# First mixture of experts: three pieces of side work take other places among the expert products

## The reference, cut to what matters

```python
def _L0_ffn_ref(x, gate_w, gate_b, w1, b1, w2, b2, gamma, beta):
    B, S, H, F, E, K = (8, 1024, 64, 128, 16, 2)
    gate_logits = x @ gate_w + gate_b
    topk_vals, topk_idx = jax.lax.top_k(gate_logits, K)
    topk_w = jax.nn.softmax(topk_vals, axis=-1)
    h = jax.nn.relu(jnp.einsum('bsh,ehf->bsef', x, w1) + b1)
    expert_out = jnp.einsum('bsef,efh->bseh', h, w2) + b2
    sel = jnp.take_along_axis(expert_out, topk_idx[:, :, :, None], axis=2)
    moe = jnp.sum(topk_w[..., None] * sel, axis=2)
    y = x + moe
    mu = jnp.mean(y, axis=-1, keepdims=True)
    var = jnp.var(y, axis=-1, keepdims=True)
    return (y - mu) / jnp.sqrt(var + EPS) * gamma + beta
...
    h = h + _L0_ffn_ref(_layernorm(h, axis=-1), ...)
    h = h + _L1_attn_ref(_layernorm(h, axis=-1), ...)
```

```python
    pos_score = (rel @ Wpos.T + bpos).transpose(2, 0, 1)
    pos_score = jax.nn.softmax(pos_score, axis=-1)
```

## Time and profile before

| | us |
|---|---|
| median of 3 runs | 759.2 (756.96 to 759.57) |
| profiled execution | 761.38 |
| its span, first to last instruction | 759.6 |
| from the first `sum_turn` (chunk 1) to the last of the eight chunks' (chunk 7) | 315.84 to 447.49 |

### The profile page before, as it was taken

One profiled execution on the slowest core, in us unless ns is written; L12 is line 12 of the kernel. 1 busy time (PEld: TensorE's weight loads), 2 busy tenths in 40 slices (PEclk: granted clock), 3 DMA queues, 4 the chain that ended last, 5 costly groups with the idle time before them and its releaser, 6 DMA issues.

```text
span 759.6 us, 16399 instructions
## 1 busy us (share of the span) xinstructions
PE 650.0 (86%) x4984; PEld 361.9 (48%) x4984; DVE 572.9 (75%) x1633; ACT 507.0 (67%) x1264; POOL 332.5 (44%) x417
## 2 busy tenths in 40 slices
PE   5528998999999988988888996788888888899896
PEld 5514655666666652333222323455555555564432
DVE  6675786777777776889988889678887888856643
ACT  3656877888888854566666767557777777734542
POOL 1006678787878857123332324634434644310000
PEclk9857999999999999999999999699999999976998
DMA  4030000000000003532223330000000000000001
GB/s 107 1 111 1 1 2 1 0 0 0 0 0 0 1 2 102 192 100 97 87 85 97 112 108 7 2 1 2 1 0 0 0 0 0 1 1 1 16 17 25
DMA packets 22038, 24.37 MB, mean 32 GB/s; under 512 B 12390, under 2 KB 12902, under 8 KB 21734
## 3 DMA queue, kind: packets, MB, share of 16 engines
q1 hardware_dynamic: 19751, 23.31, 10.0%
q10 hardware_dynamic: 2239, 0.49, 0.3%
HBM read 22.48 MB, written 1.31 MB: 31 GB/s over the span
## 4 chain that ended last, share of the span: by engine, by line
PE 58%; DVE 20%; issue 8%; ACT 4%; POOL 2%; DMA 1%; SPq 0%; DVEq 0%; ACTq 0%; POOLq 0%
PE ps L723 8%; PE ps L759 7%; PE ps L1547 5%; PE ps L641 5%; PE ps L717 4%; PE ps L652 4%; PE ps L1569 3%; DVE big L1047 3%; DVE big L1089 2%; DVE big L2054 2%; PE ps L1818 2%; PE ps L1796 2%; PE ps L705 2%; PE ps L1553 2%; PE ps L709 2%
## 5 line engine op out<-in xcount | busy, mean ns | idle before, releaser
L1334 POOL TENSOR_TENSOR big<-big 128x1024 f32<-128x1024 f32 x64 | 119.9, 1895 | 45.6 <-DVE big L1150 45.6
L937 ACT ACTIVATE big<-ps,big 128x255 f32<-128x255 f32 x256 | 117.3, 485 | 12.2 <-DVE big L1144 9.7
L901 ACT ACTIVATE big<-ps,b1s 128x512 f32<-128x512 f32 x128 | 80.5, 681 | 32.9 <-PE ps L641 32.7
L1144 DVE TENSOR_REDUCE big<-ps 128x4 f32<-128x1020 f32 x64 | 75.2, 1213 | 26.6 <-PE ps L717 26.6
L2054 DVE TENSOR_REDUCE big<-ps 128x4 f32<-128x1020 f32 x64 | 77.9, 1218 | 5.9 <-DVE res L2111 2.5
L723 PE MATMUL ps<-cst,big 128*128 128x128 f32 x512 | 76.7, 283 | 6.3 <-POOL big L1334 2.4
L652 PE MATMUL ps<-big,w2s 128*64 128x512 f32 x256 | 69.7, 623 | 9.1 <-ACT big L901 8.5
L1156 DVE COPY mid<-ps 128x512 f32<-128x512 f32 x96 | 63.4, 686 | 18.3 <-PE ps L723 15.0
L1914 ACT ACTIVATE big<-ps 128x1024 f32<-128x1024 f32 x64 | 65.8, 1029 | 14.5 <-PE ps L1559 10.0
L641 PE MATMUL ps<-big,wall 64*128 64x512 f32 x256 | 74.5, 648 | 0.7 <-ACT big L872 0.7
L723 PEld LDWEIGHTS ps<-cst,big 128*128 128x128 f32 x512 | 54.2, 140 | 40.8 <-issue 21.5
(11 more groups left out here) (274 smaller groups left out, 1351.0 us busy)
## 6 DMA issues: line engine op xcount, KB each, us to landing
mid<-spread_w SPq DMA_DIRECT2D x128, 128.0 KB, 2.8
mid<-in_split_sel SPq DMA_DIRECT2D x1, 1536.0 KB, 7.1
wall<-in_w SPq DMA_DIRECT2D x1, 1280.0 KB, 7.3
out_tokens<-res SPq DMA_DIRECT2D x16, 56.0 KB, 1.6
cst<-in_consts SPq DMA_DIRECT2D x1, 520.5 KB, 4.9
pexp<-in_w_raw SPq DMA_DIRECT2D x1, 512.0 KB, 5.4
w2s<-in_w SPq DMA_DIRECT2D x1, 512.0 KB, 3.3
mid<-in_taps ACTq DMA_DIRECT2D x1, 320.0 KB, 3.9
```

The source lines that it names most:

```text
L901: last = nc.scalar.activation(hid[e % 2][j], H1(e, j), ACT.Relu, bias=b1s[0][:, 2 * e + j:2 * e + j + 1])
L937: last = nc.scalar.activation(e_sb[r % 4][:, jj, tq, 0:NW], S[:, 2 * (r % 2) + jj, tq, 0:NW], ACT.Exp, scale=-1.0, bias=minus[r % 4][:, jj ...
L1144: nc.vector.tensor_reduce(minus[r % 4], S[:, 2 * a:2 * a + 2, :, 0:NW], AX.X, ALU.min).then_inc(s_mx, 1)
L1334: nc.gpsimd.tensor_tensor(e_sb[r % 4], e_sb[r % 4], bc(inverse[r % 4].unsqueeze(3), [P, 2, 2, 256]), ALU.mult).then_inc(s_A, 1)
```

## The change

Three moves, all in the first mixture of experts, and one wait. No instruction is added or taken away.

```diff
-            TURN_SUM, COLUMNS, LOGITS, GAP, WEIGHTS = 1, 6, 0, 2, 5
+            TURN_SUM, COLUMNS, LOGITS, GAP, WEIGHTS = 1, 6, 0, 2, 6
...
 (TensorE, duos)
+                        if e == WEIGHTS and (not known or c < CH - 1):
+                            weights(c + 1)
                         second(e, s)
...
                         if e == TURN_SUM and (not known or c >= 1):
                             sum_turn(c - 1, 1 - q, known and c == CH - 1)
-                        if e == WEIGHTS and (not known or c < CH - 1):
-                            weights(c + 1)
...
 (ScalarE, duos)
-                        if e in (4, 5) and c >= 1:
-                            own_scale(c - 1, ((0, 1), (2, 3))[e - 4])
-                        if e == WEIGHTS + 1 and (not known or c < CH - 1):
+                        if e == 5 and c >= 1:
+                            own_scale(c - 1, (0, 1))
+                        if e == WEIGHTS and (not known or c < CH - 1):
                             weights(c + 1, 1 - q)
+                        if e == 6 and c >= 1:
+                            own_scale(c - 1, (2, 3))
...
 (GpSimd, duos)
+                    if 1 <= c < CH - 1:
+                        pool.wait_ge(s_comb, c + 2)
                     for h in ((0, 1), (2,), (3,), (4,), (5,), (6,), (7,), ())[c]:
                         pos_scores(h)
```

## The result

| | before | now |
|---|---|---|
| median | 759.13 (755.28 to 760.28, 12 runs) | 749.49 (746.54 to 754.31, 12 runs) |
| profiled execution | 761.38 | 747.16 |
| its span | 759.6 | 745.3 |
| first `sum_turn` of the chunks to the last | 131.65 | 121.35 |
| from there to the end of the span | 312.1 | 308.3 |

The ratio is 0.9883, with a 95% interval of 0.986 to 0.9905. The forecast was 8.4 us less; the medians differ by 9.6. In the new kernel's profile VectorE's lines stand 2 further down (L1130 is now L1132, L1089 L1091, L1047 L1049, L1049 L1051, L1041 L1043, L1021 L1023, and GpSimd's L1290 to L1292 are L1292 to L1294). TensorE's and ScalarE's are unchanged.

A forecast was written before the change was run, and what follows sets the result against it. Waits through the spread and the turn bound a full chunk at 21.82 us; VectorE's loop would then bind at 20.41. Savings of 2.0 + 5.6 + 0.8 = 8.4 us from 759.2 gave 750.8, range 747.0 to 756.5.

The forecast's parts named there:

- PE's two idle times: In each full chunk, 1.12 us ahead of second of e = 5 and 0.97 ahead of the weights' turn, together 2.09.
- the loop of VectorE and sum_turn: VectorE's path from one sum_turn to the next: 19.72 + x = 20.41 us, taking over as a full chunk's bound.
- x: VectorE's added time per full chunk when GpSimd's moved scores meet the adds of e = 4 and e = 5: 0.69 us.
- rival on the collision: Two: GpSimd's hold-up of VectorE vanishes, 747.3 us, chance 0.12; or all 1.45 us a chunk moves, 755.2, chance 0.16.
- the collision: GpSimd's position scores slowing VectorE's spread and the instruction just ahead: 1.45 us in each of chunks 1 to 6.
- The slower rival: GpSimd's three score instructions hold VectorE throughout behind the spread, x = 2.76 us: 763.1 us, chance 0.05.
- the thin margin: ScalarE's relu of e = 7 done at C + 3.2 us, wanted by TensorE at about C + 3.4; C ends the spread.
- The entry: The entry into chunk 1, taken as unchanged: 0, with 0.3 us either way.
- the dip of chunk 4: TensorE's clock dip in chunk 4 before the change, 23.41 us instead of 21.82; the forecast left it as it was.
- the later turn: Weights' turn one product later on PE: hidden of e = 7 fills 1.06 us of the wait for the spread.
- the spread's loop: From VectorE's product of e = 2 through the spread to the turn, then PE: 21.82 us, less 1.45 and 1.06, 19.3.
- PE's own bound: PE's busy time in a full chunk, the least it could take by PE alone: 19.73 us.

The follow-up runs named there:

- e7: Changed kernel with GpSimd's position scores of heads 2 to 7 replaced by four fills that read nothing: 744.66 us, ratio 0.9836.
- e8: Changed kernel with GpSimd's position scores waiting for sum_turn instead of the spread, ahead of own_root: 742.3 us, ratio 0.9786.
- e10: Changed kernel with VectorE's last add and first logits instruction ahead of the product of e = 0, and the scores at sum_turn: 742.13 us, ratio 0.9776.
- e5: Changed kernel without GpSimd's wait, so the scores run beside the spread again: 755.99 us, ratio 0.997.
- e1: Kernel before with only GpSimd's wait added, putting the position scores behind the spread: 748.38 us, ratio 0.9873.
- e2: Kernel before with only ScalarE's new order, the relu of e = 5 ahead of own_scale: 762.46 us, ratio 1.0056.
- e3: Kernel before with only the turn of the weights moved behind hidden of e = 7 on TensorE: 754.12 us, ratio 0.9929.
- e6: Changed kernel with own_scale back ahead of the relus of e = 4 and e = 5 on ScalarE: 752.12 us, ratio 0.9906.
- e4: Changed kernel with the turn of the weights left where it was, one product earlier: 748.84 us, ratio 0.988.
- e11: The changed kernel run again, unaltered, on another chip share with two other variants: 750.71 us, ratio 0.9882.
- e9: Changed kernel with VectorE's last add of a chunk and first logits instruction ahead of the product of e = 0: 742.98 us, ratio 0.9788.

## Why the prediction was right

**What bounds the chunk.** PE's two idle times were the whole of what PE had over its work, and the three parts took both away: the earlier trace rows against PE's rows of now. The prediction did not book their sum, 2.09, but 1.41, since the loop of VectorE and sum_turn takes over at 20.41. It did, at 20.29. By its parts, in chunk 3: from sum_turn to the product of e = 2, 359.25 - 356.00 = 3.25 (forecast 3.28); from there to the product of e = 4, 365.90 - 359.25 = 6.65 (6.67); from there to the next sum_turn, 376.29 - 365.90 = 10.39 (10.46, with x). Of the 0.12 between 20.41 and 20.29, 0.07 lies in the last part, which holds x.

**x.** Forecast 0.69, from an add that ended 0.54 after GpSimd's instruction in the earlier trace rows. Measured 0.59: 0.15 instead of 0.20, 0.44 instead of 0.49. The 0.54 held to 0.01 at both adds. e7 sized x by itself (0.57 a chunk). So neither rival on the collision was right: it does not vanish, and of the 1.45 taken out of the spread 0.59 is moved, since part of the three instructions falls beside products and statistics that do not mind them.

**The slower rival** needed x of 2.1. A VectorE instruction held up once is let in when GpSimd's current one is done, and GpSimd's next then waits in turn (L1293, 1.00). In chunk 1 alone it went worse, where L1294 met the second add from its start:

```profile
327.64 1.27 POOL L1294 TENSOR_TENSOR pexp<-pexp,big 128x512 f32<-128x512 f32 x1
327.71 1.76 DVE L1091 TENSOR_TENSOR big<-big 128x512 f32<-128x512 f32 x1
```

That costs 1.08 at one add, but it does not set the chunk: e7 and e8, which have no such add, take 20.06 there, and the changed kernel 20.10.

**Chunk 1 and ScalarE.** What sets chunk 1, forecast at 19.8, is a wait that the prediction did not have. PE and then ScalarE of the changed kernel:

```profile
331.71 1.08 PE L652 MATMUL ps<-big,w2s 128*64 128x512 f32 x4 [0.43 <-ACT big L901]
```

```profile
327.08 0.76 ACT L877 ACTIVATE big<-big 128x64 f32<-128x64 f32 x2
327.75 1.23 ACT L901 ACTIVATE big<-ps,b1s 128x512 f32<-128x512 f32 x2
328.88 0.57 ACT L862 ACTIVATE big<-ps 128x512 f32<-128x512 f32 x1
...
329.85 0.49 ACT L890 ACTIVATE pexp<-pexp,pmax 128x256 f32<-128x256 f32 x1
...
330.35 2.37 ACT L901 ACTIVATE big<-ps,b1s 128x512 f32<-128x512 f32 x4
```

ScalarE has no air here from the second pair of scalings on, and in chunk 1 it also has two heads' exponentials (L890) behind the columns, so the relu of the next chunk's e = 0 comes late. The 0.43 stands in the same place in e7 to e10 (0.21 in e5), but not in the kernel before. The prediction weighed the thin margin of the new order at the relu of e = 7, which held in the chunks 1 to 5 and was missed by 0.41 in chunk 6, and not the instructions behind it.

**The sum.** Forecast 2.0 in chunk 1, 5.6 in chunks 2 to 5, 0.8 in chunk 6, in all 8.4. Measured 1.70; 4 x 1.52 = 6.1 at equal clock; 0.92; in all 8.7. That the sum is off by only 0.3 is in part luck: chunk 1 brought 0.3 less than forecast, for a reason that the prediction did not have, and the others 0.6 more, since x was smaller and the loop a little shorter. The entry was taken as unchanged and gained 0.23. The profile has 131.65 - 121.35 = 10.30 between the sum_turns, because the dip of chunk 4 (1.6), left as it was in the forecast, did not come again. The medians differ by 9.6, so about 1 us of the gain lies outside the chunks and is no part of what was forecast.

**Which part brings what.** Each alone, at equal clock, brings 1.05 (e1), 0.02 (e2) and 0.63 (e3) a chunk; left out of the whole, each is missed by 0.88 (e5), 0.48 (e6) and 0.06 (e4). The prediction had the later turn at 1.06 on the spread's loop; that loop is at 20.35 once the collision is out of it (e4), only 0.06 over VectorE's, so nothing more of the 1.06 can show.

**TensorE's clock.** Behind the last sum_turn, where only ScalarE's order in chunk 7 is changed, it took 312.1 before and 308.3 now. PE was at 1.2 GHz for 44.9 us there before and for 36.3 now, as the windows over each microsecond of that stretch add up. In the profiles of e1 to e11 the stretch takes 306.9 to 310.5, with 27 to 42 of it at 1.2 GHz, and nearly all of it is the same code in each. Such differences can be why the two profiled executions differ by 14.2 and the medians by 9.6; no run separates them. In e8 to e10 the medians gain 16 to 17 us, where the chunks at equal clock gain 11.4 to 12.7 and the lower ends of the intervals stand at 12.8 to 14.3. What makes up the rest is open: the profiles have it ahead of the first sum_turn and behind the last one, partly as less time at 1.2 GHz, and no run was made to tell why.

## What to carry to other kernels

Where several engines chase each other round a loop, write down the period of each loop, with the terms from one profile, and take the longest: it gave every kernel here within 0.16 us a chunk, while the idle times beside PE promised 2.09 where 1.53 came. When GpSimd holds up VectorE, look for a stretch in which VectorE has a wait, statistics, or products with an operand in PSUM, and put GpSimd's work there; a later place in GpSimd's queue only chooses what is hit, here two adds at 0.59 instead of the spread at 1.45. And where one loop passes through a long queue, let the instruction that releases the next engine go first: an add and a small instruction moved ahead of a product were worth 0.62 a chunk (e9), as much as removing the collision (0.57, e7).

## What the runs showed of the hardware

- An add of VectorE held up by GpSimd ended 0.54 to 0.56 after GpSimd's instruction, in six places: L1091 behind L1292, behind L1294 and behind L1294 in chunk 1, the one of 0.73 in e8, and the earlier trace rows, behind a copy of GpSimd's that ends at 457.14. That is so whatever part of the add had passed. Fills by GpSimd for 2.27 us held nothing up.
- Longer stops of PE were often followed by 1.2 GHz, within 1.6 us of their end. Of the seven stops of 2.15 us in these stages (six in e2, one in e11) five were; the chunk then took 1.5 to 1.6 us more in e2 and 3.05 in e11. Of the seven stops of 1.33 to 1.60 us ahead of the first or the last sum_turn, those of e6 (1.60) and e11 (1.44) were, and those of the changed kernel (1.43), e3 (1.41), e6 (1.33), e7 (1.58) and e8 (1.56) were not. In e1 and e3 to e6, whose stops between the first and the last sum_turn are at most 1.12, none was; in the kernel before, with 1.12 and 0.97 some 2 us apart, one chunk of six had it. That the stops are the cause is a reading of these counts.
- PE's busy time in a full chunk goes up with the number of its stops: 19.72 to 19.80 with two of them, 19.62 to 19.67 with one, 19.59 with none. Why is not shown; the profile models the ends of matmuls. The prediction took 19.73 for PE's own bound, which is 19.59 (e10).
